# First attention of the model: query mix moved from DVE to ACT and Pool, tokens one group later, products of zeros left out

## What is computed

```
def attn_a(x, Wq_d, bq_d, W_qk, b_qk, Wkv_d, bkv_d, Wv_u, bv_u, Wo, bo):   # x is normalised; 32 heads
    C_q  = x @ Wq_d + bq_d                     # 12 query latents
    C_kv = x @ Wkv_d + bkv_d                   # 4 key and value latents, shared by all heads
    q = (C_q @ W_qk + b_qk).reshape(b, s, 32, 4)
    scores = einsum('bqhd,bkd->bhqk', q, C_kv) / sqrt(4)
    attn = softmax(scores)                     # no mask
    V = (C_kv @ Wv_u + bv_u).reshape(b, s, 32, 16)
    return einsum('bhqk,bkhd->bqhd', attn, V).reshape(b, s, 512) @ Wo + bo
```

## Time and profile before

| what | value |
|---|---|
| median of 3 runs | 2277.07 us (2275.81 to 2278.4) |
| the profiled execution | 2275.74 us |
| its span, first to last instruction | 2273.9 us |
| TensorE's granted clock, mean | 0.953 |
| PE busy | 2086.4 us (92%) |
| DVE busy | 1400.9 us (62%) |
| ACT busy | 1164.6 us (51%) |
| POOL busy | 824.2 us (36%) |
| the attention's own costliest row: L1440, 128 maxima | 151.9 us, 1219 ns each |
| L1569, 256 products by key | 91.2 us, 512 ns each |
| L1581, 192 products of zeros | 32.8 us, 281 ns each |
| L1430, 16 query mixes | 12.0 us, 750 ns each |

### The profile page before, as it was taken

One profiled execution on the slowest core, in us unless ns is written; L12 is line 12 of the kernel. 1 busy time (PEld: TensorE's weight loads), 2 busy tenths in 40 slices (PEclk: granted clock), 3 DMA queues, 4 the chain that ended last, 5 costly groups with the idle time before them and its releaser, 6 DMA issues. The chain is left out here.

```text
span 2273.9 us, 33298 instructions
## 1 busy us (share of the span) xinstructions
PE 2086.4 (92%) x11568; PEld 1485.0 (65%) x11568; DVE 1400.9 (62%) x2517; ACT 1164.6 (51%) x2691; POOL 824.2 (36%) x996
## 2 busy tenths in 40 slices
PE   5999987999999999999987789999999887899988
PEld 3333345777888888888765667777777574654457
DVE  5788564536666666666646456666665565567756
ACT  4677543245656656656535455555555433235553
POOL 0000100235645645545520254555445213247611
PEclk9899978999999999999999799999999987989999
DMA  3000022671112112111011433443333003543301
GB/s 116 1 1 1 5 76 74 193 232 38 46 39 66 46 39 66 44 41 47 20 38 49 123 93 91 112 109 91 99 95 96 34 19 94 163 70 76 73 24 38
DMA packets 95427, 157.77 MB, mean 69 GB/s; under 512 B 11727, under 2 KB 33359, under 8 KB 93086
## 3 DMA queue, kind: packets, MB, share of 16 engines
q1 hardware_dynamic: 85662, 134.26, 20.6%
q0 software_dynamic: 9600, 21.38, 3.9%
HBM read 90.58 MB, written 31.46 MB: 54 GB/s over the span
## 5 line engine op out<-in xcount | busy, mean ns | idle before, releaser
L2528 POOL TENSOR_TENSOR attn1a_probs<-attn1a_probs,attn1a_recip 128x128 f32<-128x128 f32 (+3 forms) x256 | 178.9, 720 | 234.6 <-DVE attn1a_recip L2711 234.0
L1889 POOL TENSOR_TENSOR attn0b_probs<-attn0b_probs,attn0b_recip 128x128 f32<-128x128 f32 (+3 forms) x256 | 196.1, 787 | 184.9 <-DVE attn0b_recip L2133 184.9
L2584 ACT ACTIVATE attn1a_probs<-attn1a_scores,attn1a_negmax 128x128 f32<-128x128 f32 (+3 forms) x256 | 132.7, 523 | 175.4 <-DVE attn1a_negmax L2697 174.1
L1993 ACT ACTIVATE attn0b_probs<-attn0b_scores,attn0b_negmax 128x128 f32<-128x128 f32 (+3 forms) x256 | 132.7, 524 | 122.3 <-DVE attn0b_negmax L2126 121.7
L1440 DVE TENSOR_REDUCE attn0a_negmax<-attn0a_by_query 128x2 f32<-128x1024 f32 x128 | 151.9, 1219 | 11.8 <-PE attn0a_by_query L1557 11.8
L2697 DVE TENSOR_REDUCE attn1a_negmax<-attn1a_scores 128x2 f32<-128x256 f32 (+3 forms) x128 | 105.4, 823 | 71.4 <-PE attn1a_scores L2886 71.3
L1882 POOL TENSOR_TENSOR attn0b_q_cos<-attn0b_q_cos,attn0b_q_swap 128x512 f32<-128x512 f32 x64 | 84.3, 1317 | 159.9 <-DVE attn0b_q_swap L2115 159.9
L2001 ACT ACTIVATE attn0b_probsT_hi<-attn0b_turned 128x256 fp32r<-128x256 f32 (+3 forms) x128 | 90.1, 704 | 88.2 <-PE attn0b_turned L2277 86.6
L2126 DVE TENSOR_REDUCE attn0b_negmax<-attn0b_scores 128x2 f32<-128x256 f32 (+3 forms) x128 | 105.0, 820 | 46.7 <-PE attn0b_scores L2266 46.7
L2898 PE MATMUL attn1a_turned<-ident_f,attn1a_probs 128*128 128x128 f32 x640 | 116.1, 279 | 8.6 <-DVE attn1a_probsT L2705 7.3
L2112 DVE TENSOR_TENSOR attn0b_q_cos<-attn0b_aux,attn0b_cos_q 128x512 f32<-128x512 f32 x60 | 41.5, 691 | 116.2 <-ACT attn0b_q_swap L2014 116.2
(11 more groups left out here) (509 smaller groups left out, 6249.5 us busy)
## 6 DMA issues: line engine op xcount, KB each, us to landing
pre<-in_b_o SPq DMA_DIRECT2D x16, 1024.0 KB, 5.4
attn1a_qT<-attn1a_stage SPq DMA_DIRECT2D x128, 128.0 KB, 2.4
attn1a_qT<-attn1a_stage SPq DMA_DIRECT2D x64, 256.0 KB, 3.8
attn0b_vals<-attn0b_v_out SPq DMA_DIRECT2D x16, 512.0 KB, 3.9
attn0b_keys<-attn0b_part SPq DMA_DIRECT2D x32, 256.0 KB, 4.2
pre<-in_b_q SPq DMA_DIRECT2D x8, 1024.0 KB, 7.6
attn0b_kT<-attn0b_keys SPq DMA_DIRECT2D x64, 128.0 KB
pre<-in_b_kv SPq DMA_DIRECT2D x5, 1024.0 KB, 6.8
```

The costliest lines, as they stand in the source:

```text
L1889: pool.tensor_tensor(x, x, recip[:, r % DEEP, e:e + 1].broadcast_to([P, (qt + 1) * P]), ALU.mult).then_inc(s_scaled, 1)
L1993: act.activation(probs[:, r % DEEP, e, 0:width], scores[r % 2][:, e, 0:width], ACT.Exp, bias=negmax[:, r % 2, e:e + 1], accum_out=sums[:, ...
L2528: pool.tensor_tensor(x, x, recip[:, r % DEEP, e:e + 1].broadcast_to([P, (qt + 1) * P]), ALU.mult).then_inc(s_scaled, 1)
L2584: act.activation(probs[:, r % DEEP, e, 0:width], scores[r % 2][:, e, 0:width], ACT.Exp, bias=negmax[:, r % 2, e:e + 1], accum_out=sums[:, ...
```

## The change

- `query_rest`, a new float32 tile of two buffers. ACT writes it right behind `query_part` (from `aux`, times the other factor per row) for steps 1 to 15, and tells it with a new semaphore `s_qrest`. 
- Pool adds `query_rest` and `query_part` into `queries` for these steps. DVE's `mix_queries` at g = 3 goes; only that of step 0 is left on DVE.
- PE's transposes of tokens into `aux` wait for `s_qrest` where they waited for the mix.
- DVE's `to_tokens` moves from g = 5 to g = 6.
- `add_zeros`, its tile, its memset and its semaphore go: 192 products.

```diff
-        query_part = n.sb("query_part", [P, 2, SEQ], F32R)
+        query_rest, query_part = n.sb("query_rest", [P, 2, SEQ]), n.sb("query_part", [P, 2, SEQ], F32R)
-        zeros, s_zeros = n.sb("zeros", [P, P], BF16), n.sem("zeros")
@@ gpsimd
-            pool.memset(zeros[:, :], 0.0).then_inc(s_zeros, 1)
             pool.memset(negmax[:, :, :, :], 0.0).then_inc(s_ones, 1)
+
+            def mix_queries(step):
+                pool.wait_ge(s_qpart, step + 1)
+                pool.wait_ge(s_qrest, step)
+                if step >= 2:
+                    pool.wait_ge(s_shifted, step - 1)
+                pool.tensor_tensor(queries[:, step % 2, :], query_rest[:, step % 2, :],
+                                   query_part[:, step % 2, :].bitcast(F32), ALU.add).then_inc(s_q, 1)
+
+            for step in range(1, STEPS):
+                mix_queries(step)
@@ scalar, signed_queries
                 act.activation(query_part[:, step % 2, :], aux_flat, ACT.Copy, scale=row_kind[:, 2:3])\
                     .then_inc(s_qpart, 1)
+                if step >= 1:
+                    act.activation(query_rest[:, step % 2, :], aux_flat, ACT.Copy, scale=row_kind[:, 3:4])\
+                        .then_inc(s_qrest, 1)
@@ vector
-            def mix_queries(step):
-                dve.wait_ge(s_qpart, step + 1)
-                dve.scalar_tensor_tensor(queries[:, step % 2, :], aux_flat, row_kind[:, 3:4],
-                                         query_part[:, step % 2, :].bitcast(F32), ALU.mult,
-                                         ALU.add).then_inc(s_q, 1)
+            def mix_first_queries():
+                dve.wait_ge(s_qpart, 1)
+                dve.scalar_tensor_tensor(queries[:, 0, :], aux_flat, row_kind[:, 3:4], query_part[:, 0, :].bitcast(F32),
+                                         ALU.mult, ALU.add).then_inc(s_q, 1)
...
-                    if g == 3 and step + 1 < STEPS:
-                        mix_queries(step + 1)
...
-                    if g == 5 and step >= 2:
+                    if g == 6 and step >= 2:
                         to_tokens(step - 2)
@@ tensor, aux_free
-                    pe.wait_ge({"Q": s_q, "M": s_shifted, "T": s_out}[kind], step + 1)
+                    if kind == "Q" and step >= 1:
+                        pe.wait_ge(s_qrest, step)
+                    else:
+                        pe.wait_ge({"Q": s_q, "M": s_shifted, "T": s_out}[kind], step + 1)
...
-            def add_zeros(first=None):
-                if first is not None:
-                    if first >= 1:
-                        pe.wait_ge(s_osb, first)
-                    else:
-                        pe.wait_ge(s_v, 1)
-                for _ in range(3):
-                    pe.matmul(out[:, 0:2, :].rearrange("v t q -> v (t q)"), zeros[:, :],
-                              m.mask[:, :, :].rearrange("p e x -> p (e x)"), start=first is not None,
-                              stop=first is not None)
...
-            pe.wait_ge(s_zeros, 1)
...
-                    if g == 3 and 1 <= step <= STEPS:
-                        add_zeros(first=step - 1)
-                    if g in (5, 7) and 1 <= step <= STEPS or g == 1 and step >= 2:
-                        add_zeros()
```

More of the change, by code:

```diff
@@ L1244, in attn0a_block @@
             n.sem(k) for k in ("wo", "bias_v", "merged", "merged_hi", "both_biases")]
-        s_aux, s_qpart, s_q, s_shifted = [n.sem(k) for k in ("aux", "qpart", "q", "shifted")]
+        s_aux, s_qrest, s_qpart, s_q, s_shifted = [n.sem(k) for k in ("aux", "qrest", "qpart", "q", "shifted")]
         s_by_query, s_max, s_by_key, s_exp = [n.sem(k) for k in ("by_query", "max", "by_key", "exp")]
@@ L1469, in split_merged @@
                                   ALU.subtract).then_inc(s_merged_hi, 1)
-            mix_queries(0)
+            mix_first_queries()
             dve.wait_ge(s_ones, 1)
```

## The result

| | before | after |
|---|---|---|
| median | 2277.74 us (2275.81 to 2282.03, 4 runs) | 2326.07 us (2324.41, 2325.92, 2326.22) |
| the profiled execution | 2275.74 us | 2324.41 us |
| its span | 2273.9 us | 2322.7 us |
| mean granted clock | 0.953 | 0.925 |
| end of the attention | 280.6 us | 325.5 us |

The changed kernel is slower by 2.1%: the ratio is 1.0209, with the interval 1.0193 to 1.0226. The forecast was no change, so it is wrong by 48 us, and far outside of its range. (A fourth execution of the changed kernel took 5173.96 us, with a granted clock of 1.0; nothing on record explains it, and it is left out.)

The account below looks back on a forecast made before the run. The attention was taken as bound by a path between PE and ACT, with DVE's work off it in steady steps. Terms -0.66 + 0.53 + 1.95 - 1.0 = +0.8 us took the median 2277.07 to 2277.9 us, range 2275 to 2281.

Parts of the forecast that it names:

- The path and the sum at full clock: PE and ACT path, steps 2 to 14: new copy less group 1 zeros, 0.15 us a step, +1.95; whole sum +0.8.
- Step 0: DVE's query mix there precedes five maxima without a gap; its removal was to gain 0.66 us.
- Pool's addition: Pool adding query_rest and query_part: nearest row 1281 ns, wanted some 5 us later, cost 0, at most 0 to 0.1.
- DVE's work removed and tokens later: Steady steps: nobody waits for the 0.75 us mix, gain 0; to_tokens a group later, gain 0 to 0.03 a step.
- Rival B: Zeros of group 1 are covered anyway, so the copy costs 0.53 in each step: 4.9 us more, 2282.8; chance 0.10.
- rival C: DVE or the zeros are on the path: -9.9 us (2267) if DVE, -17 if the zeros; chance 0.13.
- The tail: Steps 16 and 17, without scores: three groups of zeros on PE's path go, -1.0 us (-0.7 to -1.3).
- the change of tile: Part of the up to 0.43 us each group of zeros holds PE; about 0.1 stays after their removal.
- rival A: The clock falls in the steps without zeros: 0.25 us per us at 1.2 GHz, 2289 to 2325 and more; chance 0.13.
- a quarter: Clock rival's case of a quarter of the 175 us at the low clock: costs 11 us, 2289.

Follow-up runs that it names:

- the third copy: Kernel before without zeros, plus an extra ACT copy of aux behind the query copy into an unread tile, DVE's mix kept: 2284.74, 2291.47, 2326.36 and 2326.92 us.
- first experiment: Kernel before with only the 192 products of zeros left out: 2282.82 us, ratio 1.0025.
- second copy two groups later: Changed kernel, still without zeros, with ACT's query_rest copy moved behind the exponentials of group 4: 2278.37 us, ratio 1.0009.

## Why the prediction was wrong, point by point

*The path and the sum at full clock: right.* The prediction had 0.10 to 0.21 us a step; a full-clock step of the same path is 13.69 us with the zeros of group 3 alone and 13.68 with the third copy, against 13.47, so +0.21 to +0.22, the upper end. Its two halves were measured apart: the zeros of group 1 gave back 0.37 (forecast 0.36 to 0.38), the copy takes 0.57 from start to start (227.23 to 227.80), or 0.59 in the length of the step (forecast 0.48 to 0.57). by_key of group 2 is no longer held by zeros: it starts 0.65 behind its exponential (224.50 to 225.15 in the order of time above), forecast 0.67. *Step 0*: -0.66 forecast; the query copies of steps 0 and 1 are 13.17 us apart and were 13.83: -0.66. *Pool's addition*: 1265 ns (forecast 1281), and nobody waits for it:

```profile
L1295 POOL TENSOR_TENSOR attn0a_queries<-attn0a_query_rest,attn0a_query_part x15: 1263/1265/1272, 47.7 to 279.3; 128x512 fp32r<-128x512 f32 x15
```

That the addition costs DVE nothing was an estimate. It holds here: in the changed kernel the 17 maxima that one of the additions overlaps take 1215 to 1227 ns and the 111 others 1215 to 1228, and `shift` takes 691 to 692 ns (690 to 692 before). L2120 is another matter: in the kernel before, it takes 680 to 683 ns in the eight times that Pool does nothing beside it, and 735 to 1254 where Pool works all through it.

*DVE's work removed and tokens later*: nothing gained; DVE waits for by_query instead, 45.2 us, and the steps are 13.10 us with DVE's mix (first experiment) and without it (second copy two groups later). *Rival B* (zeros of group 1 covered) fell with the first experiment, and so did the half of *rival C* that had all zeros on the path: 13.10 us, not 12.8 or less. Its other half, DVE on the path, fell with the pair just named. *The tail*, -1.0, can't be read from the changed kernel, where the clock falls in it. The kernel with the late second copy and the zeros of passes 1 to 3 has no zeros in the tail and the clock at 1.00 to the end of the attention: from DVE's `shift` of pass 16 to its last `to_tokens` it takes 19.33 us (253.50 to 272.83), and 20.41 in the kernel before (259.94 to 280.35), -1.08. The 0.1 for the change of tile is borne out at the place of rows 3: the three products of zeros start 0.11 to 0.12 us apart, and by_key 0.20 behind the last of them, 0.09 more.

*Slips in its numbers.* The low ends of the terms add up to -0.3, not -0.7; two and a half parts in the tail at 0.43 less 0.1 make -0.8, not -1.0. "With products of 32 rows only" isn't so: from 54.58 us four transposes of all 128 rows are in that stretch, and the stretch with 12.93 busy of 13.60 us has products of zeros and products by values of 128 rows. No trace gives a figure in GHz; the granted clock is read as 0.50 and 1.00 of full speed, at which a product of zeros takes 421 and 273 ns (median, 60 to 69 and 100 to 240 us of the kernel before). None of this decides the outcome.

*The argument against rival A: wrong.* This is the step that failed: the sum put the clock's part at nothing, on the ground that "nothing as thin is in a step", and measured it is 133.1 us more at a clock of 0.50, some 45 us. Rival A was named, with its mark in the trace, and given 0.13. That its end value ("all of them ... 2325 and more") is near the measured 2326.07 is in part luck: its own price of 0.25 for 175 us makes 44, or 2321 us; in fact fewer microseconds were low, each at a higher price. Three reasons stood against it, and each failed in its own way.

First, "the zeros are 24 of 153 us of PE's busy time" is a mean over twelve steps. The clock fell behind one place of a step, and there they were 0.50 us and stood in the hole itself. The removal of the zeros and the longer hole fall together at that place; the prediction costed both edits there (at group 3: "nothing") and did not put them side by side.

Second, "nothing as thin is in a step", against the 1.50 of 3.40 us ahead of the fall at 281.2, was read off a step of the kernel before, with the zeros in it and without the new copy. The step of after could have been worked out from the rows: by_key comes 1.72 us behind the query copy (143.03 to 144.75), and one more copy of 0.57 makes it 2.29, which is what after shows (226.66 to 228.95); without the zeros in between, all of what was their place and the copy's 0.57 is idle time. The 2.03 busy of 3.40 us that comes of it lies nearer to the 1.50 than to the 2.84 of 3.40 that stood there.

Third, one fall was taken as one price. At 0.50 PE becomes the bound (busy 9.52 of 10.20 us from 230.80), which is seen in ACT's and DVE's waits for it (32.8 and 45.2 us from 92 to 262). In the locked cycle each step has one fall: 17.07 - 13.69 = 3.38 us for 10.24 us at 0.50, 0.33 for each. Over the attention it is 45.0 us for 133.1 more, 0.34. The price in the prediction was 0.25, from steps 1 and 2, where part of the low stretch is one in which PE waits for DVE. The count, not the price, was the bigger miss in the middle case: "a quarter" was a guess.

In short: the cause, shown by undoing each part, is in the clock, and what brings it down is the pair of a third copy in a row on ACT (moving one of them away undoes it: 2278.37 us) and the missing products in the hole it makes (putting zeros back undoes that: 15 us left). Alone, the missing zeros cost 7 us in spite of shorter steps, with a later rise of the clock, and the copy 15 us, about half of it by longer steps. The pair is not enough by itself each time, as the third copy with DVE's mix kept shows (two of four executions fell); what tips it is not shown.

## What to carry to other kernels

Before work on PE that computes nothing is taken out, look for where it stands, not for how much it is: lay out one step with all edits of the change in it, find the longest idle time of PE, and compare what is left around it with what stood ahead of a fall anywhere in the trace. This is a warning sign and no bound, since here equal busy times stood ahead of a fall and of none. Work moved to an engine with time to spare belongs where no one waits behind it: the same copy two groups later in the same queue was worth 48 us. And where a kernel has a low clock early and holds it later, the filler may be needed for the rise alone; here the zeros of three passes did for the clock of the steps what those of all had done, in a kernel whose steps have no hole of over 0.8 us.

## What the runs showed of the hardware

- PE's filler of 32 rows did not hold the clock as filler of 128 rows did: 2326 us and more in three of four executions against 2283 to 2296 in six of six, with the same count of products and columns, and falls behind stretches in which PE was busy 2.52 and 2.63 of 3.40 us.
- A kernel can have two outcomes that are 40 us apart: the third copy (2284.74 and 2291.47, or 2326.36 and 2326.92) and the 32-row zeros (2287.05, or 2326 and more). In the changed kernel, from 190 us to the end of the scores, the cycle of the clock and the step have the same length, 17.07 us.
- Executions of one kernel differ by some 6 us either way without any change (2276.53 to 2289.01 in the ten of the kernel without zeros), and their mean granted clock goes with it: 0.951 at 2276.53 us, 0.943 at 2289.01. A single pair of profiles can't show 5 us here, and gains of this size in one block, as the 7.5 us above, needn't reach the total.
